# The third low part of each strip: from VectorE to GpSimd, in a two-layer convolution kernel

## The reference, cut to what matters

```python
xm = einsum('bchw,oc->bohw', x, W_in)                 # 32 -> 3 * 85 channels
x_spatial, x_freq, x_gate = split(xm, 3, axis=1)
out_spatial = depthwise_conv_3x3(x_spatial, W_dw)     # SAME padding
xf = rfft2(x_freq in 8x8 patches) * fft_weight        # (85, 1, 1, 8, 5)
out_freq = irfft2(xf) back in place
x_fused = gelu(x_gate) * (out_spatial + out_freq)
return einsum('bchw,oc->bohw', x_fused, W_out)        # 85 -> 32 channels
```

## Time and profile before

| | |
|---|---|
| median of 3 runs (lowest, highest) | 836.8 us (836.58, 837.75) |
| the profiled execution | 836.89 us, of which 835.1 us is the span of the trace |
| TensorE's mean granted clock | 0.997 of full speed |
| PE busy | 799.8 us, 96% of the span |
| DVE busy | 609.3 us, 73% |
| ACT busy | 568.7 us, 68% |
| POOL busy | 270.8 us, 32% |

### The profile page before, as it was taken

How to read it: one execution, slowest core, us unless ns; L and a number is a source line. 1 busy time by engine, 2 the same in 40 slices (tenths; PEclk the granted TensorE clock), 3 DMA queues, 4 the chain that set the end, 5 groups by cost and what they waited for, 6 DMA issues and landing times.

```text
span 835.1 us, 31399 instructions
## 1 busy us (share of the span) xinstructions
PE 799.8 (96%) x12324; PEld 653.7 (78%) x12324; DVE 609.3 (73%) x1153; ACT 568.7 (68%) x1149; POOL 270.8 (32%) x349
## 2 busy tenths in 40 slices
PE   1599999999999999999999999999999999999997
PEld 0388888877887878887888888888888888888885
DVE  6788787887887876787777776677666767667553
ACT  1376767676667677777776777777777776776664
POOL 1724322443235423243334323332233232232221
PEclk9999999999999999999999999999999999999999
DMA  7667557556555456565446565555656555566521
GB/s 273 167 166 211 127 119 209 121 123 139 120 130 116 103 123 137 129 139 118 106 108 137 136 152 142 140 134 140 147 145 158 138 137 139 145 141 151 146 69 51
DMA packets 66458, 115.51 MB, mean 138 GB/s; under 512 B 16242, under 2 KB 18858, under 8 KB 65930
## 3 DMA queue, kind: packets, MB, share of 16 engines
q1 hardware_dynamic: 63654, 110.11, 53.7%
q0 software_dynamic: 2272, 2.72, 1.4%
q10 hardware_dynamic: 388, 0.69, 0.3%
HBM read 10.98 MB, written 8.56 MB: 23 GB/s over the span
## 4 chain that ended last, share of the span: by engine, by line
PE 93%; DVE 4%; ACT 1%; issue 1%; DMA 1%; DVEq 0%; ACTq 0%
PE ps_s L390 34%; PE ps_ft L430 14%; PE ps_o L439 8%; PE ps_g L396 6%; PE ps_u L396 5%; PE ps_z L462 5%; PE ps_s L470 4%; PE ps_s L471 4%; PE ps_s L473 4%; PE ps_z L465 4%; PE ps_z L463 4%; DMA x<-in_x 1%; PE ps_ft L379 1%; DVE st L733 1%; DVE parts L815 1%
## 5 line engine op out<-in xcount | busy, mean ns | idle before, releaser
L390 PE MATMUL ps_s<-cw,stack 128*128 128x85 f16 (+1 forms) x7168 | 456.8, 203 | 0.0
L390 PEld LDWEIGHTS ps_s<-cw,stack 128*128 128x128 f16 (+1 forms) x7168 | 378.6, 98 | 49.0 <-DVE f L880 0.7
L633 POOL TENSOR_TENSOR yl<-y,yh 128x340 f16<-128x340 f32 x256 | 224.2, 876 | 532.5 <-ACT yh L573 532.0
L573 ACT ACTIVATE yh<-y 128x340 f16<-128x340 f32 x256 | 124.6, 487 | 200.3 <-DVE y L912 138.1
L906 DVE SCALAR_TENSOR_TENSOR ul<-ps_u,uh 128x340 f16<-128x340 f32 x256 | 129.8, 507 | 103.3 <-ACT uh L564 102.3
L815 DVE TENSOR_TENSOR parts<-xn,parts 128x1024 f16<-128x1024 f32 (+2 forms) x99 | 117.8, 1194 | 93.3 <-ACT parts L525 93.3
L430 PE MATMUL ps_ft<-squares_sb,f 128*85 128x128 f32 x1024 | 162.6, 281 | 1.3 <-ACT ft L558 1.1
L558 ACT ACTIVATE ft<-ps_ft 85x512 f32<-85x512 f32 x256 | 149.0, 582 | 19.8 <-PE ps_ft L430 17.0
L568 ACT ACTIVATE g<-ps_g,gsc 128x340 f32<-128x340 f32 x256 | 137.3, 536 | 1.2 <-PE ps_g L396 1.0
L880 DVE TENSOR_TENSOR f<-ps_s,g 128x340 f32<-128x340 f32 x256 | 128.7, 503 | 12.5 <-PE ps_s L473 4.0
L912 DVE TENSOR_TENSOR y<-ps_z,weff 128x340 f32<-128x340 f32 x256 | 128.1, 500 | 1.4 <-PE ps_z L465 1.4
(11 more groups left out here) (86 smaller groups left out, 600.5 us busy)
## 6 DMA issues: line engine op xcount, KB each, us to landing
stack<-parts SPq DMA_DIRECT2D x496, 130.0 KB, 2.5
out_y<-yo SPq DMA_DIRECT2D x16, 512.0 KB, 2.9
stack<-parts SPq DMA_DIRECT2D x124, 65.0 KB, 2.1
stack<-parts SPq DMA_DIRECT2D x124, 64.5 KB, 2.1
stack<-parts SPq DMA_DIRECT2D x124, 64.0 KB, 2.0
x<-in_x SPq DMA_DIRECT2D x3, 2048.0 KB, 10.2
x<-in_x SPq DMA_DIRECT2D x4, 512.0 KB, 6.9
gathered<-sums POOLq DMA_DIRECT2D x28, 24.0 KB, 2.2
```

The lines of the kernel that those rows point to most:

```text
L390: mm(ps_s[i % 2][:, HID * q:HID * (q + 1)], pixels(kind, i, q, dy, rows), w[0:rows, m, :], start=(q == 0 and m == 0), stop=False)
L573: nc.scalar.activation(yh[:, i % 2, :], y32[:, i % 2, :], ACT.Copy).then_inc(s_yh, 1)
L633: nc.gpsimd.tensor_tensor(yl[:, k, :], y32[:, k, :], yh[:, k, :], ALU.subtract).then_inc(s_yl, 1)
```

## The change

POOL gets a `lo_part` of its own, and calls it in step 6 for the strip under preparation, ahead of its `yl` of that step. DVE's part 6 is left out wherever `i >= 0`; in the prologue (`i < 0`, strip 1) DVE still makes all three. The waits are the ones that DVE's version had, and one more: POOL waits until the second low part has been counted in `s_xl`, so that the count still goes up in order. The shift is `ORDER[-1]`, that is -1.

```diff
@@ in pool's program @@
+            def lo_part(strip, dx):
+
+                pool.wait_ge(s_xn, norms(strip))
+                pool.wait_ge(s_xh, splits(strip, ORDER.index(dx)))
+                pool.wait_ge(s_xl, splits(strip, ORDER.index(dx) - 1))
+                part = parts[strip % 2][:, :, 1 + dx, TW:TW + SW].rearrange("p a (r w) -> p a r w", w=TW)
+                nc.gpsimd.tensor_tensor(part[:, LO], xn[:, :, 1 + dx:1 + dx + TW], part[:, HI],
+                                        ALU.subtract).then_inc(s_xl, 1)
+
             for i in steps():
+                strip, last = staged(i, {6: 6})
+                if i >= 0 and last:
+                    lo_part(strip, ORDER[-1])
                 if live(i, 2):
                     k = i % 2
                     need(pool, s_s, i + 1)
@@ in dve's program @@
                 for part in mine:
                     if part == 0:
                         norm(strip)
-                    else:
+                    elif i < 0 or part < 6:
                         lo_part(strip, ORDER[part // 2 - 1])
```

## The result

The changed kernel took 841.35 us (median of 6 runs, 840.01 to 842.92) against 836.69 us (6 runs, 836.33 to 837.75): 4.7 us more, ratio 1.0054 with a 95% interval of 1.0040 to 1.0068. It is slower, beyond what can be mistaken for no change, and just above the upper end of the range, 841.2.

A forecast was written before the change was run, and what follows sets the result against it. PE, busy 96% of the span, was taken to bound the kernel, waiting for DVE only at step 5's tiles. Ordinary strips 0.0 and four gather strips +1.2 on the 836.8 us median gave 838.0 us, range 835.6 to 841.2.

The forecast's parts named there:

- What bounds the kernel: Steady loop: PE waits for DVE only at step 5's tiles, 3.8 us in all; the removed instruction is not before that wait.
- The price of the instruction: POOL's new third low part of 1024 elements in step 6: 2.4 us each, bounded between 2.0 and 3.25.
- Ordinary strips cost nothing: In ordinary strips POOL's new instruction ends 2.3 us before norm starts, covered up to 4.7 us long: cost 0.0.
- The four gather strips: After gathers in steps 37, 69, 101 and 133 the low part starts late and holds up norm: +1.2 us in all.
- 0.3 us late. Four such strips: +1.2 us: PE's spectrum of step 41 starts at 167.2 instead of 166.88, taken alike for four gather strips.
- 1.1 us late: DVE's edge column behind norm ends at 166.3 instead of 165.19, and y32 of step 40 is late by as much.
- Rival 2: Small inverse-root instructions after y32 in steps 14, 46 and 78 are locked out 1.4 us each: 840.1 us; chance 0.18.
- Rival 3: POOL far slower on runs of 8, from 4.7 us per low part, making norm late everywhere: 843 to 849; chance 0.08.
- rival 4: DVE's freed time reaches PE, removing half of the 3.8 us of late step 5 tiles: 834.9 us; chance 0.10.
- Rival 1: Everything is hidden, the gather strips included: 836.8 us; chance 0.26.
- DVE busy near 572: DVE's busy time after losing 30 instructions of 1.226 us, 36.8 us in all: about 572 us.

The follow-up runs named there:

- second: Kernel before, with POOL making the second low part (step 4); DVE keeps the third: 835.46 us, ratio 0.9978.
- skip4: Changed kernel, but DVE makes the third low part in steps 38, 70, 102 and 134, POOL in the other 26 strips: 836.95 us, ratio 0.9993.
- the second trace: The changed kernel run once more, unaltered, for another trace: 842.01 us, ratio 1.0043.
- delay4: Kernel before, with two unused statistics instructions (about 1.3 us) on DVE after norm in steps 40, 72, 104 and 136: 841.23 us, ratio 1.0046.
- later_gather: Changed kernel, all 30 low parts on POOL, with the statistics collection of steps 36, 68, 100 and 132 one step later: 836.81 us, ratio 0.9996.
- the dummy: Kernel before, with an unused 1020-element multiplication on POOL ahead of yl in steps 38, 70, 102 and 134: 838.78 us, ratio 1.0017.

## Why the prediction was wrong

- *What bounds the kernel*: right in the main. PE waits for DVE around step 5 (three tiles of step 6 are late by 0.07 as well), and the third low part is not in front of that wait. second and skip4 show both halves of it.
- *The price of the instruction*, 2.4 us: 2.15. The Trainium skill's rule ("GPSIMD Engine Reference", Performance versus the Vector engine) gave an estimate of 2.2; the trace agrees.
- *Ordinary strips cost nothing*: right, in 26 places. skip4 has them at 836.95.
- *The four gather strips*: the right place, and the right kind of path (lock, late `y32`, late spectrum in tile 41), wrong size. **The step that failed is "0.3 us late. Four such strips: +1.2 us"**: measured 1.17, 0.52, 1.8 and 0, that is 3.5 us in all, and 3.0 in the second trace. Four things are in it. First, I followed the lateness to the next tile and stopped, as if DVE caught up. delay4 shows that a lateness of 1.16 us reaches PE whole, 0.47 at once and 0.69 at steps 4 and 5. I had the evidence and did not use it: a tile of step 5 that is late already, as 206.15 is the earlier trace rows, says that the loop of DVE and ACT has no slack in that strip. In the four strips at hand the tile of step 5 was late before the change by 0.49, 0.64, 0.37 and 0.00 us, and only the last cost nothing. Second, DVE's weights instruction of step 39 stood in the queue ahead of `norm`, and I priced only `norm` and its edge column. Third, I took the gather's issue time of one trace for all: at step 101 it came 1.2 us late, as its DMA had not landed. Fourth, I priced one strip and multiplied by four, where the lateness of `y32` was 1.16, 0.52, 1.73 and 0.88. The fourth strip absorbed it: it is in layer 1, the second layer, which has no statistics in step 3 and whose tiles of step 5 are on time.
- *"1.1 us late" in step 40*: 1.16 us, near by luck. It was added up from a held `norm` and a held edge column, and these ran at 0.87 and 0.40 us; the lateness came from the weights instruction, 1.4 us longer than before.
- *The rest of this trace*: 1.2 us at tiles 12 and 13, 0.3 ahead of tile 0 and 0.26 given back had no term in the sum.
- *Rival 2* falls. The two small instructions after `y32` ran at full speed in the middle of POOL's low part (step 14, 86.96 to 89.12); POOL's row first, then DVE's:

```profile
86.96 2.16 POOL L634 TENSOR_TENSOR parts<-xn,parts 128x1024 f16<-128x1024 f32 x1
87.55 0.27 DVE L783 TENSOR_SCALAR nr<-nr,ve 128x1 f32<-128x1 f32 x1
...
87.85 0.15 DVE L787 TENSOR_SCALAR nr<-nr 128x1 f32<-128x1 f32 x1
```

- *Rival 3* falls (2.15 us), and so does *rival 4*: skip4 gives back 0.1 us at the late tiles of step 5. later_gather gives back 1.3 there and loses 0.8 at tiles 46 and 78, and its median is that of the kernel before. *Rival 1* is what skip4 and later_gather make true. The outcome is "slower", to which I gave 0.36.
- *DVE busy near 572*: 582.8. Longer instructions make up some 6 us of the difference, and 4 come from taking the page's busy time for a sum of durations.

Open: how much of the third place is `norm`'s wait and how much is the lock; and whether the loss at tiles 12 and 13 comes more often with the change. Seven of the twelve traces at hand have a low part on POOL ahead of these tiles; two of them show it, and two of the five others do, which is too few to tell.

## What to carry to other kernels

Before a small delay is written off against one wait's slack, look at the tightest point of the next round: here, where the engines that release each other were already late there, the delay was paid almost in full, part of it later, whichever instruction of the queue had caused it. The instruction moved to an idle engine was free in the ordinary rounds; its price was in the few rounds in which that engine had something else to do, so those are priced first, each by itself. And of several like pieces of work, the one to move is the one in front of the wait: the second low part gave 1.8 us, the third gave nothing even where it did not collide (skip4, later_gather), and took 4.7 where it did.

## What the runs showed of the hardware

- Some VectorE instructions and GpSimd's arithmetic shut each other out for whole instructions, as the Trainium skill has it for the ports that the two share ("SBUF — State Buffer", Who interferes with whom). `norm` took 1.34 us for 0.87 behind a `yl`, and the next `yl` took 1.39 for 0.83 behind that `norm`. A VectorE instruction with two inputs in SBUF is shut out too (2.42 us for 1.22). The [128,1] instructions, of the same operation as `norm`, are not (0.27 and 0.15 us in the middle of a 2.16 us GpSimd instruction).
- The 255-element instruction did not get in between two of POOL's: it took 1.76 us with two `yl` behind the low part, 1.76 with one, and 1.34 with two `yl` behind the dummy, each time until POOL's run of ready work was over. `norm` did not always get in either. It began 0.11 us behind the low part in steps 104 and 136 alike; in step 104 it ran between the two `yl` (1.34 us), in step 136 behind both (2.09 us), and the second trace shows the same pair (1.34 and 2.09). What decides who goes next was not tried. Step 136 of the first trace:

```profile
465.96 1.62 POOL L645 TENSOR_TENSOR yl<-y,yh 128x340 f16<-128x340 f32 x2
466.12 2.09 DVE L803 TENSOR_SCALAR xn<-x,mv,rstd 128x1152 f32<-128x1152 f32 x1
```

- The landing time of one 24 KB statistics DMA, that of step 8, varied from 2.6 to 6.6 us over the twelve traces. Where it was long, GpSimd's queue stood behind it (4.48 us at 6.6).
